# Three edits to a six-part perceiver kernel: tile order and start of the first stage, value projection in the token attentions, unrolled expert turns

## The reference, cut to what matters

```python
# x: (8, 128, 512), ctx: (8, 2048, 512)
x = x + swishmax_attention(layernorm(x), ctx)        # 8 heads; part "swishmax"
x = x + twin_attention(layernorm(x))                 # 16 heads, softmax(A1) - lambda * softmax(A2); part "twin"
h = layernorm(x); m = h + plain_attention(g1 * layernorm(h) + b1)              # part "plain"
x = x + m + experts(g2 * layernorm(m) + b2)          # part "experts"
x = x + cross_attention(layernorm(x), ctx)           # part "context"
x = x + feature_attention(layernorm(x))              # part "features"
x = x + per_feature_nets(layernorm(x))               # part "nets"

def swishmax_attention(q_tokens, ctx):               # per batch and head
    logits = (ctx @ key_down) @ (q_tokens @ query_down + bias).T
    xe = logits * exp(logits - max)                  # over the 2048 keys
    attn = xe / (sum(abs(xe)) + 1)
    return sum over heads of ((attn.T @ ctx) @ value_down) @ value_up

def experts(t):                                      # 8 experts, each 512 -> 256 -> 512
    gate = t @ Wg; take the best two; probs = softmax of the two
    return sum over experts of weight * (relu(t @ W1[e]) @ W2[e])
```

## Time and profile before

| what | value |
|---|---|
| time, median of 3 runs | 4212.75 us (4211.9 to 4213.85) |
| profiled execution: its own time | 4211.15 us |
| profiled execution: its span, first to last instruction | 4209.3 us |
| TensorE busy | 4053.0 us, 96% |
| VectorE busy | 2247.2 us, 53% |
| ScalarE busy | 1401.1 us, 33% |
| GpSimd busy | 427.8 us, 10% |
| mean granted clock of TensorE | 0.989 |

### The profile page before, as it was taken

How to read it: one execution, slowest core, us unless ns; L and a number is a source line. 1 busy time by engine, 2 the same in 40 slices (tenths; PEclk the granted TensorE clock), 3 DMA queues, 4 the chain that set the end, 5 groups by cost and what they waited for, 6 DMA issues and landing times. The chain is left out here.

```text
span 4209.3 us, 69698 instructions
## 1 busy us (share of the span) xinstructions
PE 4053.0 (96%) x28288; PEld 2813.3 (67%) x28288; DVE 2247.2 (53%) x4773; ACT 1401.1 (33%) x3796; POOL 427.8 (10%) x407
## 2 busy tenths in 40 slices
PE   8999999999999999999899999999999999999897
PEld 4777777777777777677465444666666666666675
DVE  4455555554545455255544334666666666656556
ACT  2222222222222222144333101444444444444343
POOL 2020202020202020022210000000000000000222
PEclk9999999999999999999999999999999999999999
DMA  4111111111111112201211400101101101101000
GB/s 141 61 61 61 61 61 61 61 61 61 61 61 61 61 61 71 86 22 40 105 41 41 165 0 25 51 14 56 54 14 55 55 14 54 44 11 44 11 2 21
DMA packets 123701, 219.55 MB, mean 52 GB/s; under 512 B 9088, under 2 KB 47616, under 8 KB 121600
## 3 DMA queue, kind: packets, MB, share of 16 engines
q1 hardware_dynamic: 110208, 166.91, 12.0%
q0 software_dynamic: 13184, 48.24, 3.6%
HBM read 198.35 MB, written 16.78 MB: 51 GB/s over the span
## 5 line engine op out<-in xcount | busy, mean ns | idle before, releaser
L583 PE MATMUL swishmax_attended<-swishmax_weights_t,swishmax_context 128*128 128x128 f32 x4096 | 522.1, 276 | 0.0
L583 PEld LDWEIGHTS swishmax_attended<-swishmax_weights_t,swishmax_context 128*128 128x128 f32 x4096 | 492.7, 193 | 14.8 <-issue 14.8
L1508 PE MATMUL context_bank<-ahead_stream,ahead_staged 128*128 128x512 f32 x1024 | 473.0, 605 | 1.3 <-PEq L1081 1.3
L597 PE MATMUL swishmax_bank<-ahead_stream,ahead_w 128*128 128x512 f32 x1024 | 463.8, 596 | 7.6 <-DMA ahead_stream<-in_context_t_dram 7.6
L1374 ACT ACTIVATE context_exps<-context_score,context_neg_max 128x512 f32<-128x512 f32 x512 | 344.7, 685 | 378.3 <-DVE context_neg_max L1406 378.3
L441 ACT ACTIVATE swishmax_xes<-swishmax_score,swishmax_neg_max 128x512 f32<-128x512 f32 x256 | 177.3, 694 | 843.2 <-DVE swishmax_neg_max L476 843.2
L583 PE MATMUL swishmax_attended<-swishmax_weights_t,swishmax_sides 128*128 128x128 f32 x3072 | 385.5, 275 | 0.0
L1406 DVE TENSOR_REDUCE context_neg_max<-context_score 128x1 f32<-128x512 f32 x512 | 317.8, 684 | 104.1 <-PE context_score L1476 103.3
L1508 PEld LDWEIGHTS context_bank<-ahead_stream,ahead_staged 128*128 128x128 f32 x1024 | 184.2, 189 | 280.8 <-issue 274.0
L583 PEld LDWEIGHTS swishmax_attended<-swishmax_weights_t,swishmax_sides 128*128 128x128 f32 x3072 | 364.4, 192 | 0.0
L476 DVE TENSOR_REDUCE swishmax_neg_max<-swishmax_score 128x1 f32<-128x512 f32 x256 | 164.8, 686 | 349.5 <-PE swishmax_score L568 349.5
(11 more groups left out here) (341 smaller groups left out, 5529.9 us busy)
## 6 DMA issues: line engine op xcount, KB each, us to landing
ahead_stream<-in_context_t_dram SPq DMA_DIRECT2D x78, 1024.0 KB, 5.6
swishmax_context<-in_context_dram POOLq DMA_DIRECT2D x32, 1024.0 KB, 5.9
swishmax_down<-_L_xattn_value_down_dram SPq DMA_DIRECT2D x64, 256.0 KB, 3.4
swishmax_up<-in_L_xattn_value_up_dram SPq DMA_DIRECT2D x32, 512.0 KB, 5.0
ahead_values<-ahead_staged SPq DMA_DIRECT2D x14, 1024.0 KB, 8.9
context_values<-ahead_values POOLq DMA_DIRECT2D x56, 256.0 KB, 3.5
experts_w<-in_L_ffn_W_dram SPq DMA_DIRECT2D x16, 512.0 KB, 8.0
whole_x<-in_x_dram SPq DMA_DIRECT2D x8, 256.0 KB, 10.9
```

What stands on the lines that cost most here:

```text
L583: last = nc.tensor.matmul(product(i)[:, m, :], side(left, c, k, m), weights_t[:, n % 2, right, k, :], start=c == 0 and k == 0 and m == 0 a ...
L597: last = nc.tensor.matmul(bank_t[:], w_key[:, k, g * P:(g + 1) * P], context_t[:, c, k, :], start=k == 0, stop=k == DC - 1)
L1508: last = nc.tensor.matmul(bank_t[:], w["k"][:, k, g * P:(g + 1) * P], context_t[:, c, k, :], start=k == 0, stop=k == DC - 1)
```

## The change

1. In the first part `inner` and `output` stand behind the `attend` of their step in TensorE's list, and behind the scaling in VectorE's. Up to step `n = LAG` the key tile stands ahead of both turned halves, on ScalarE behind both exps and ahead of the turned half. `stats` 1 moves from step n = 4 to n = 1, and SP loads the rows of x ahead of context chunks 2 and 3.
2. In the token attentions TensorE's `value` stands between `heads` and `output`, and ScalarE evicts it at the slot's end, behind all exps.
3. The experts' loops are written out. The turn's normalisation becomes `set_tokens`: four instructions of each kind in a row. For turn 2 it is called in turn 1, ahead of the eviction of inner tile 5. The means are read from `rows_of_mid.mv`, so that their copy goes.

```diff
             out = [("key", 0, c + 1)] * (u == 0 and c + 1 < NCH) + [("score", u, c)] * (u < NU)
-            out += [("turned", u - 1, c, 0)] * (1 <= u <= NU) + [("key", u + 1, c)] * (u + 1 < NU) + [("turned", u - 1, c, 1)] * (1 <= u <= NU)
+            key, turned = [("key", u + 1, c)] * (u + 1 < NU), [("turned", u - 1, c, r) for r in range(HG)] * (1 <= u <= NU)
+            out += key + turned if n <= LAG else turned[:1] + key + turned[1:]
+            out += [("attend", (n - LAG) // NCH, (n - LAG) % NCH)] * (0 <= n - LAG < NU * NCH)
             out += [("inner", (n - LAG) // NCH - 1)] * (n - LAG >= NCH and (n - LAG) % NCH == 0)
             out += [("output", (n - LAG) // NCH - 1)] * (n - LAG >= NCH and (n - LAG) % NCH == 1)
-            out += [("attend", (n - LAG) // NCH, (n - LAG) % NCH)] * (0 <= n - LAG < NU * NCH)
             return out + [("hidden", b + 1)] * (g == 2 and c == 1 and b + 1 < B) + [("query", b + 1)] * (g == 2 and c == 2 and b + 1 < B)
...
             out = [("key", 0, c + 1)] * (u == 0 and c + 1 < NCH)
-            out += [("exp", u, c, 0)] * (u < NU) + [("turned", u - 1, c, 0)] * (1 <= u <= NU)
-            out += [("exp", u, c, 1)] * (u < NU) + [("key", u + 1, c)] * (u + 1 < NU)
+            key, turned = [("key", u + 1, c)] * (u + 1 < NU), [("turned", u - 1, c, 0)] * (1 <= u <= NU)
+            if n <= LAG:
+                out += [("exp", u, c, r) for r in range(HG)] * (u < NU) + key + turned
+            else:
+                out += [("exp", u, c, 0)] * (u < NU) + turned + [("exp", u, c, 1)] * (u < NU) + key
             out += [("abs", u, c, r) for r in range(HG)] * (u < NU)
...
             out += [("turned", u - 1, c, 1)] * (1 <= u <= NU)
-            out += [("inner", (n - LAG) // NCH - 1)] * (n - LAG >= NCH and (n - LAG) % NCH == 0)
-            out += [("output", (n - LAG) // NCH - 1)] * (n - LAG >= NCH and (n - LAG) % NCH == 1)
             if c < NCH - 1:
...
                 out += [("combine", u), ("scale", u, 0)] * (u < NU)
+            out += [("inner", (n - LAG) // NCH - 1)] * (n - LAG >= NCH and (n - LAG) % NCH == 0)
+            out += [("output", (n - LAG) // NCH - 1)] * (n - LAG >= NCH and (n - LAG) % NCH == 1)
             out += [("values", (n - LAG) // NCH, 1)] * (n - LAG >= 0 and (n - LAG) % NCH == NCH - 1)
-            out += [("stats", 1)] * (n == NCH) + [("norm", b + 1)] * (g == 1 and c == 2 and b + 1 < B)
+            out += [("stats", 1)] * (n == 1) + [("norm", b + 1)] * (g == 1 and c == 2 and b + 1 < B)
             return out + [("hidden", b + 1)] * (g == 2 and c == 1 and b + 1 < B) + [("query", b + 1)] * (g == 2 and c == 2 and b + 1 < B)
...
                 load(sp, w_key[:, :, P:], a["key_down"][:, P:], w_loaded["key"])
+                for b in range(1, B):
+                    sp.dma_start(x_sb[:, b, :], x_dram[b]).then_inc(x_loaded, 16)
                 for c in range(2, NCH):
                     load_context_t(0, c)
-                for b in range(1, B):
-                    sp.dma_start(x_sb[:, b, :], x_dram[b]).then_inc(x_loaded, 16)
...
             out += [("score", t - 1, 1)] * (c and SETS == 2)
-            out += ([("key", t, n) for n in range(STREAMS)] + [("value", t, 0)]) * p
-            return out + [("heads", t - 2, 0), ("output", t - 2, 0)] * o + at_end(t)
+            out += [("key", t, n) for n in range(STREAMS)] * p + [("heads", t - 2, 0)] * o
+            return out + [("value", t, 0)] * p + [("output", t - 2, 0)] * o + at_end(t)
...
             out += [("query", t, n) for n in range(STREAMS)] * p
-            out += [("exp", t - 1, 1, 0), ("exp", t - 1, 1, 1)] * (c and SETS == 2)
-            out += [("value", t, 0)] * p
-            return out + [("exp", t - 1, 1, 2), ("exp", t - 1, 1, 3)] * (c and SETS == 2) + at_end(t)
+            out += [("exp", t - 1, 1, r) for r in range(SR)] * (c and SETS == 2)
+            return out + [("value", t, 0)] * p + at_end(t)
...
-        means = s.sb("means", [P, B])
...
-        LINKS = 2 * NB + 10
...
                     nc.scalar.copy(ahead.staged[:, j % 2, :, k, :], spare_ring.bank(t)[:].rearrange("p (g d) -> p g d", d=P)).then_inc(out_s, 1)
-                with act.Fori(0, TURNS) as i:
+                for i in range(TURNS):
                     for t in ring_a.at:
...
                 rows_of_mid.take(nc, first, range(B), mid)
-                first(nc.vector.tensor_copy(means[:], rows_of_mid.mv[:, :, 0]))
                 dve.wait_ge(loaded, 16 * LOADS)
                 dve.wait_ge(added, B)
-                with dve.Fori(0, TURNS) as i:
-                    link = Chain(dve, chain, LINKS, i)
+                link = Chain(dve, chain)
+
+                def set_tokens(i):
                     for n in range(NB):
-                        b = i * NB + n
-                        link(nc.vector.tensor_scalar(tokens[:, n, :], columns(mid, b), tile_at(means, b), tile_at(rows_of_mid.rstd, b),
-                                                     ALU.subtract, ALU.mult))
-                        link(nc.vector.tensor_tensor(tokens[:, n, :], tokens[:, n, :], gain[:], ALU.mult))
+                        last = rows_of_mid.apply(nc, tokens[:, n, :], i * NB + n, mid)
+                    link(last)
+                    for n in range(NB):
+                        last = nc.vector.tensor_tensor(tokens[:, n, :], tokens[:, n, :], gain[:], ALU.mult)
+                    link(last)
+                    for n in range(NB):
                         nc.vector.tensor_tensor(tokens[:, n, :], tokens[:, n, :], offset[:], ALU.add).then_inc(normed_x, 1)
+
+                set_tokens(0)
+                for i in range(TURNS):
                     for n in range(NB):
...
                     dve.wait_ge(out_d, ring_d.landed(i, ("gate", NB - 1)))
-                    link.hold()
                     for n in range(NB):
...
                     link(last)
-                    link.hold()
                     for n in range(NB):
...
                     for f in range(1, FT, 2):
+                        if f == 5 and i + 1 < TURNS:
+                            dve.wait_ge(out_a, ring_a.landed(i, ("token", NB - 1)))
+                            set_tokens(i + 1)
                         t = ("inner", f)
...
                                 dve.wait_ge(out_d, ring_d.landed(i, ("expert", n, e - 1)))
-                            acc = columns(x_sb, i * NB + n)
+                            acc = x_sb[:, i * NB + n, :]
                             nc.vector.scalar_tensor_tensor(out=acc, in0=ring_d.bank(t)[:], scalar=weight[:, n, e:e + 1], in1=acc,
                                                            op0=ALU.mult, op1=ALU.add).then_inc(out_d, 1)
-                    link.close()
...
                 pe.wait_ge(loaded, 16 * LOADS)
-                with pe.Fori(0, TURNS) as i:
+                for i in range(TURNS):
                     for t in steps:
```

4 lines of the change are left out of this document (removed).

## The result

The changed kernel takes 4138.31 us (median of 4 runs, 4137.65 to 4141.67), the kernel before beside it 4213.3 (4 runs, 4211.9 to 4214.43). The ratio is 0.9824, 95% interval [0.9807, 0.9841]: 75 us less. The profiled execution took 4137.65, its span is 4135.9.

The account below looks back on a forecast made before the run. TensorE, busy 96% of the span, bounds the kernel; only about 156 us idle and slow stretches can be won. Terms 35.3 + 9.4 + 10.4 + 5.3 + 10.5 = 70.9 off 4211.15 give 4140 us, range 4130 to 4157.

Parts of the forecast that it names:

- Part 1: First stage: inner and output tiles behind the attended product save 1.16 us a unit, 35.3 us; bounds 20 and 38.
- Rival A: First stage: waits only change their name, the key tile behind waits for VectorE; gain near 0, total 4175; chance 0.06.
- Part 2: Start of the kernel: moved key tiles, statistics and x loads save net 9.4 us; bounds 5 and 12.
- That is 2 us too little: Start: VectorE's 5.4 us gap is short for the statistics; chunk 2's maximum slips 2.0, chunk 3's score some 0.9.
- The two new waits on the key copy: Start, steps 5 and 6: second turned tile takes the key tile's bank, emptied after both exps; 2.1 and 0.9 us.
- The loads of x ahead of two context chunks: Start: chunk 2 lands some 4.8 us later, still in time; cost nothing, without that cover at most 4.8.
- rival B: Start gains nothing and twin's heads copy is late: Part 2 at 0, Part 3 at 8, total 4152; chance 0.10.
- Part 3: Token attentions: value projection between heads and output saves 10.4 us over both stages; ScalarE's new order saves 5.3.
- The cover of 0.3 us: Twin stage: heads copy done near 1949.8, TensorE through at 1950.1; if not enough, a few tenths each return.
- Part 4: Experts: with turns unrolled and normalisation moved, turn 2 looks like turn 1; saves 10.5 us, bounds 9 and 12.2.
- Rival D: Experts: unrolled turns change nothing, the wait returns as a stall for instructions; total 4151; chance 0.04.
- The upper bound of 12.2: Experts, turn 2: the saving in us if the clock drop seen in turn 1, worth 1.7, does not occur.

Follow-up runs that it names:

- Run 2: Changed kernel, with GpSimd's first sums waiting on a semaphore until VectorE's statistics (left in the second step) are done: 4140.24 us.
- run 3: Changed kernel with the statistics back in the fifth step (n = 4), new order of loads and of key and turned tiles kept: 4143.81 us.
- 4: Changed kernel with its whole start undone (statistics in the fifth step, x loads behind the context chunks, old tile order): 4143.8 us.
- run 8: Changed kernel with the first inner tile of each expert turn between the second and third gate product: 4134.45 us.
- run 1: Changed kernel with the statistics of batches 1 to 7 in the first step (n = 0), not the second: 4137.42 us.

## Why the prediction was right, and where it was not

**Part 1: right.** Steps of 13.60, 13.49 and 11.77, no wait on either tile, none on the key tile behind. 36.9 us in its stretch against 35.3: 30 units by 0.67 + 0.50 = 1.17 make 35.1, and of the 2.82 us of one late wait for the values before, 1.11 stayed. Rival A is out. At the end the first wait for the values stayed, 2.32, as the text said. Undoing it cost 38.7 - 1.7 = 37.0 as well.

**Part 2: wrong, 0.1 in place of 9.4.** The step that failed is "the statistics stand in step 2, where VectorE idled 5.4 us ... That is 2 us too little". The gap was read rightly, the 7.4 us to be put in it were taken from a place where GpSimd was idle (its last sum there ended at 51.0, the statistics began at 59.97). In step 2 the GpSimd row (the last sum of the first chunk, ending at 33.40, with three chunks to come) already said that GpSimd would be working there, and I used that row only to ask whether its sums are ready in time. The statistics took 15.4 us there, so the maximum of chunk 2 began at 48.39 where it had begun at 40.07, and the score of chunk 3 waited 8.6, with the clock at its lower level for 10.2 us from 44.8 on, 4.3 of them behind the wait. Run 2 shows the cause by moving GpSimd alone. The Trainium skill has the rule ("SBUF — State Buffer", section "Who interferes with whom"): a VectorE instruction with two SBUF inputs, or one in a 2-port mode, and a GpSimd instruction that reads SBUF need the same port pair; whoever comes first holds it for its whole instruction, and the other is blocked. By that rule a small instruction that begins inside a sum waits for its end, at most 1.27 us, and instructions with one SBUF input outside those modes wait for nothing. The trace agrees: five of the slow instructions took 1.11 to 1.24 and ended with the sum they began in, two scalings took 2.97 in place of 0.88, and the statistics instructions of L158 4.24 against 4.25. It leaves open the 1.50 and 1.99 of the two that began during the issue of a fetch. (The text's sum of new costs has a slip as well: 0.9 + 2.1 + 0.9 + 0.4 is 4.3, not 4.2.)

The two new waits on the key copy were expected at 2.1 and 0.9 and measured 1.26 and 0.40; the new orders of tiles and loads lost 3 us together (run 3 against 4). The loads of x ahead of two context chunks cost nothing in the way that was forecast: no key tile waited for a chunk but the first, and the first chunk's sums, begun at 32.00 and done at 37.3, were 33 us early for the attended product at 70.83. That all of GpSimd's sums run 4 us later by them, and so beside other work of VectorE, the text did not price. Half of rival B is therefore what happened; its other half, the twin heads copy, did not.

**Part 3: right, 17.8 for 15.7.** Each of twin's six slots with a projection became 1.2 us shorter, not 0.86: the products of heads, value and output 0.9, and the turned tiles 0.3, which stood before on ScalarE's eviction of an `ahead` tile. ScalarE's new order is the likely reason for the 0.3, but no run has it alone. The score wait of 3.57 is gone with its clock drop. The cover of 0.3 us for the copy in twin was enough. Both waits at the end stayed, 6.13 and 0.85.

**Part 4: the term of 10.5 was mis-sized, 8.9.** Turn 2 looks as forecast in its idle time (none), but the low clock at the gate lasts 6.8 us, not 3.4. By stretch it is 9.1, and undoing it costs 10.1. Rival D is out. The upper bound of 12.2 stood for a turn without a drop, and run 8 then gave that: 15.55 less 12.19 is 3.4 more, 12.3 with the 8.9. The sentence of the Trainium skill ("TensorE: Matmul & The Clock Gate", section on the HAM clock gate) that activity releases the throttle can't be read as recorded busy time: TensorE was recorded busy throughout in both kernels, and the clock fell in one and not in the other.

**Why the total was still right.** 70.9 less the 9.3 that did not come, plus 1.6 and 2.1 and less 1.1 on the other parts, is 64.2. To the 73.4 of the spans 9.2 are missing: 1.6 ahead of the first score, 3.2 where the 13.7 us drop after the first stage did not come in this execution, 4.4 at the end of the kernel, most of it clock as well. Low clock in all: 98.2 us before, 65.1 after, some 16 us of work. Of this only the drops at the start, at the twin score and at the experts' gates were in the sum, none of these three places; in other kernels with all four parts' gains (run 1) the drop was there and the total came out the same through a better start. The total being near is luck to the size of this sum, the signs and places of parts 1, 3 and 4 are not.

## What to carry to other kernels

Before work is moved into an idle gap of VectorE, look at what GpSimd does in that gap: here a small instruction on SBUF operands that began inside one of GpSimd's sums ended only with that sum, so a chain of small ones was the worst to put there, while the long statistics instructions (L158) kept their time. A price read from a row is the price beside the neighbours of that row. And when edits are worth less than 5 us, read each in its own stretch from anchor to anchor: totals move by as much through clock drops that fall differently.

## What the runs showed of the hardware

- In a chain of thirteen VectorE instructions on 128x7, 0.17 us each when GpSimd was idle, seven took 1.1 to 2.0 beside GpSimd sums of 1.27 us, and each ended 0.01 to 0.04 us behind a sum's end. Two 128x512 scalings took 2.89 to 2.97 in place of 0.88. The sums themselves took 1.25 to 1.29 beside the small instructions and up to 1.44 beside the large ones.
- Seven statistics instructions on 128x512 (L158) took 4.24 beside the same sums and 4.25 without them; maxima and weightings that read PSUM stayed at 0.69.
- 32 gapless matmuls of eight columns came with 3.4 or 6.8 us at the lower clock in 16 of 18 places; 16, a full tile, and 16 with none in 8 places.
- The same idle times ahead of the same tiles were followed by no drop there and 3.4 us later in the profiled executions of four kernels, and by 10.2 or 13.7 us in those of eight others.
